# The last two turns of a pipelined transformer block written as a part of their own, with expert weights summed on TensorE

## The chip, the cores and the metric

The kernel runs on one core of one Trainium2 chip. The metric is the device time in microseconds of one execution; lower is better. Engines are named as in the profile: PE is TensorE (PEld its weight loads), DVE is VectorE, ACT is ScalarE, POOL is GpSimd and SP is the queue that issues DMAs.

## What is computed

For each of 32 batches of 256 tokens of width 128: a modulated layer norm, causal attention with 16 heads of 64 and a gated output, a residual, a second modulated layer norm, and a feed-forward part which is the sum of a gated MLP of 512 and of product-key experts. Only the experts matter here:

```python
q = (h @ Wq).reshape(b, t, 2, H, RET // 2)            # H = 4
sim = jnp.einsum('btphn,hkpn->pbthk', q, keys)        # 64 keys on each of 2 axes
sc, ix = jax.lax.top_k(sim, 8)                        # 8 of each axis
all_sc = sc[0][..., :, None] + sc[1][..., None, :]    # 64 sums, best 8 kept: scores, idx
w = silu(einsum('btd,bthkd->bthk', h, down_embed[idx])) * softmax(scores)
experts = einsum('bthk,bthkd->btd', w, up_embed[idx]) # 512 experts (NEXP)
x = x + gb * (mlp + experts)
```

## The kernel before

The 32 batches are software-pipelined. Each engine runs `body(i)` for i = -1 to 33; turns 3 to 30 are a hardware loop, the others are written out. In turn i attention works on batch i, the output projection, second norm and key similarities on f = i - 1, and the experts and the MLP on g = i - 2. So in turn 32 (i = B) there is no attention left: it finishes batch 31 up to its similarities and batch 30 wholly; turn 33 has the expert part of batch 31 alone. In both, the engines run their normal list of steps with those left out whose batch doesn't exist.

In each engine the order of the steps is the order of the calls in its list. Semaphores join the engines. Work in PSUM goes through four banks `pW[0..3]`, dealt by the list `order`: job n takes bank n modulo 4, and each job waits for the release of the one before it in its bank (`wait_free`, `filled`, `wait_full`, `release`, `wait_released`). PSUM tile `pS` holds the attention scores.

The experts are computed without a gather, over all 512 of them. With exponentials `ex` of the shifted similarities, GpSimd makes for each half batch k and head h the outer product `fsum` (8 x 64 = 512 values, `products`, L422), and from the exponentials `tops` of the best eight on each axis 20 candidates (`candidates`, L411 to L416). VectorE takes the best eight of them, their sum `zz` and its reciprocal `rz` (`thresholds`, L936 to L939). Then:

- `choose` (L948, VectorE): mask times `rz`, that is (fsum >= eighth best) * rz, into `fexp`;
- `weigh` (L431, GpSimd): `fexp` times `fsum`; `add_heads` (L438, L441): the sum over the four heads, `wsum`;
- `total` (L604, ScalarE): the sum of `wsum` over the experts, `tot`; `fold` (L447, L451, GpSimd): puts 4 - tot on the last expert and multiplies `d_t` (the silu of h times the down table, `down_tanh` L579 on ScalarE and `gated_down` L857 on VectorE) by `wsum`;
- `transpose_experts` (L1184, TensorE), its copy `eT` (`experts`, L530, ScalarE), and `project_ffn` (L1193 the MLP, L1196 the experts) into `y`; `finish` (L958, L963, VectorE) writes `yo`, which SP stores.

GpSimd also does `add_bias` (L483: `x2g`, after which SP may load the next `modB`, which `ln2_stats`, L892 to L903, needs) and `rstd2` (L473, L475), between which and `h2` (L910, `ln2_modulate`) the last batch's similarities wait. `h2` is transposed, modulated (`modulate_h`, L622), split (L630, L876) and multiplied with the keys (`similarity`); `shift` (L921, L923, L926) and `expert_exp` (L592, L598) make `ex` and `tops`. GpSimd's list in a turn is: `candidates`, `products(0)`, `products(1)`, `weigh(0)`, `add_bias`, `add_heads(0)`, `fold(0)`, `rstd2`, `weigh(1)`, `rstd1`, `add_heads(1)`, `rms1`, `fold(1)`.

Of the kernel before, what the change touches and what calls it, by code (L numbers as in the profile page):

```python
# [39 lines left out]
NW = 4  # L40
# [6 lines left out]
def program(nc, x, norm_w, Wq, Wkv, Wout, Wgate, fWg, fbg, fWu, fbu, fWd, fbd, fWq, keys,  # L47
            down, up, cond, wmod, out):
    ctx = ExitStack()
    with ctx:  # L50
# [100 lines left out]
        eT = sb("eT", [P, TB, EC, P])  # L151
        yo = sb("yo", [P, TB, D])
# [19 lines left out]
        mods_stored = sem("mods_stored")  # L172

# [60 lines left out]

        class Work:
# [17 lines left out]

            def bank(self, name, k=0):
                return pW[bank_of[name, k]]
# [12 lines left out]
            def wait_free(self, name, k=0, after=(), off=None):  # L268

                need = {}  # L270
                prev = self.before(name, k)
                for pn, pk, turn in [(*j, off) for j in after] + ([prev] if prev else []):
                    key = self.key(pn, pk)
                    need[key] = max(need.get(key, (turn, 0)), (turn, place[pn, pk] + 1))
                for key, (turn, n) in need.items():
                    e = work_free[key]
                    self.eng.wait_ge(S(e), at(e, self.i + turn, n))

            def filled(self, ins, name, k=0):
                ins.then_inc(S(work_full[self.key(name, k)]), 1)  # L280

            def wait_full(self, name, k=0, b=None):
                e = work_full[self.key(name, k)]
                self.eng.wait_ge(S(e), at(e, self.batch(name, k) if b is None else b, place[name, k] + 1))

            def release(self, ins, name, k=0):
                ins.then_inc(S(work_free[self.key(name, k)]), 1)

            def wait_released(self, name, k=0, b=None):

                e = work_free[self.key(name, k)]
                self.eng.wait_ge(S(e), at(e, self.batch(name, k) if b is None else b, place[name, k] + 1))
# [5 lines left out]
        def den(p):  # L298

            return pS[:, p % 2, :, SW:SW + TB]  # L300

# [183 lines left out]


# [19 lines left out]
        def _(act):  # L506
# [17 lines left out]
            def body(i):  # L524
# [99 lines left out]
                def high_part(high, parts, name):  # L624
                    if w.has(name):
# [4 lines left out]
                        nc.scalar.copy(parts[0][:, :], w.bank(name)[:, 0:N]).then_inc(S(high), 1)  # L630

# [332 lines left out]


# [48 lines left out]
        def _(pe):  # L1014
# [43 lines left out]
            def body(i):  # L1058
# [120 lines left out]
                def transpose_experts(k):  # L1179
                    if w.has("ET", k):  # L1180
                        pe.wait_ge(S(eo_ready[k]), at(eo_ready[k], g, 1))
# [5 lines left out]
                def project_ffn(k):  # L1187
                    if w.has("y"):
# [8 lines left out]
                        if k == TB - 1:  # L1197
                            w.filled(ins, "y")

# [83 lines left out]
```

## Time and profile before

| | us |
|---|---|
| median of 3 runs | 1504.97 |
| lowest and highest run | 1503.06, 1506.31 |
| the profiled execution | 1505.26 |
| its span, first to last instruction | 1503.5 |
| busy: PE, DVE, ACT, POOL | 1408.8, 1350.8, 1247.7, 1083.3 |
| mean granted TensorE clock | 0.981 of full |

The page cuts the span in 40 slices of 37.6 us, so the last two turns are about its last two slices. The profiled execution is one of its own, 0.3 us above the median; what the trace gives is set against its span.

### The profile page before, as it was taken

The numbers are of one execution on the slowest core, as the hardware profiler recorded it, in microseconds if no ns is written. First come the engines' busy times: TensorE is split into PE (matmuls) and PEld (weight loads), VectorE is DVE, ScalarE is ACT, GpSimd is POOL, SyncE is SP. The second block draws the span as 40 slices with busy tenths as digits, with TensorE's granted clock in tenths as the row PEclk, the third lists the DMA queues.
The fourth block names the chain that finished last, engine by engine and source line by source line (L and its number), as shares of the span: only waits on it lengthen the run. The fifth ranks groups of instructions, "written<-read, shape, count | busy, mean of one in ns | idle before, by whom it ended". The sixth has DMA issues, their size and how long they took to land.

```text
span 1503.5 us, 39396 instructions
## 1 busy us (share of the span) xinstructions
PE 1408.8 (94%) x11363; PEld 1153.2 (77%) x11363; DVE 1350.8 (90%) x5371; ACT 1247.7 (83%) x4106; POOL 1083.3 (72%) x1201
## 2 busy tenths in 40 slices
PE   6799999999999999999999999999999999999953
PEld 4678788878878887877887787888788788887743
DVE  4689999999999999999999999999999999999853
ACT  4788888898888888888888888888988888898821
POOL 0237787777778777777877777787777787777786
PEclk9999999999999999999999999999999999999976
DMA  4000000000000000000000000000000000000000
GB/s 124 19 14 20 11 14 19 19 17 18 14 9 19 19 19 16 19 14 9 19 19 19 16 19 14 9 19 19 19 16 18 9 15 19 19 16 13 12 9 6
DMA packets 50736, 27.73 MB, mean 18 GB/s; under 512 B 10288, under 2 KB 49904, under 8 KB 50704
## 3 DMA queue, kind: packets, MB, share of 16 engines
q1 hardware_dynamic: 50464, 26.91, 6.7%
q10 hardware_dynamic: 240, 0.43, 0.1%
q8 instruction: 15, 0.25, 0.1%
q14 instruction: 17, 0.14, 0.0%
HBM read 23.02 MB, written 4.31 MB: 18 GB/s over the span
## 4 chain that ended last, share of the span: by engine, by line
PE 61%; DVE 24%; issue 6%; ACT 5%; POOL 3%; DVEq 0%; DMA 0%; SPq 0%; POOLq 0%
PE pS L1115 9%; PE pW L1051 9%; PE pW L1053 7%; PE pW L1052 7%; PE pW L1128 6%; PE pS L1105 5%; DVE h L910 5%; DVE pS L828 4%; PE pS L1101 4%; ACT pS L548 4%; PE pW L1193 4%; PE pW L1196 4%; PE pW L1132 2%; DVE p_sb L848 2%; PE pW L1184 2%
## 5 line engine op out<-in xcount | busy, mean ns | idle before, releaser
L548 ACT ACTIVATE pS<-pS,nmx 128x128 f32<-128x128 f32 (+1 forms) x1024 | 391.2, 440 | 54.0 <-DVE nmx L828 54.0
L431 POOL TENSOR_TENSOR fexp<-fexp,fsum 128x512 f32<-128x512 f32 x256 | 321.0, 1288 | 80.0 <-DVE fexp L948 80.0
L828 DVE CUSTOM_DVE_ANT_0 pS<-pS,mask 128x128 f32<-128x128 f32 (+1 forms) x1024 | 330.0, 389 | 21.2 <-PE pS L1105 20.5
L422 POOL TENSOR_TENSOR fsum<-ex 128x512 f32<-128x512 f32 x256 | 258.0, 1045 | 0.0
L540 ACT COPY pT<-pS 128x768 f32<-128x768 f32 x256 | 211.7, 827 | 35.4 <-PE pS L1115 31.5
L1115 PE MATMUL pS<-ident,p_sb 128*128 128x128 f32 x1536 | 216.2, 277 | 10.4 <-DVE p_sb L848 6.4
L848 DVE TENSOR_TENSOR p_sb<-pS,coef 128x256 f32<-128x256 f32 (+2 forms) x512 | 210.4, 452 | 8.9
L1115 PEld LDWEIGHTS pS<-ident,p_sb 128*128 128x128 f32 x1536 | 172.9, 141 | 41.5 <-issue 14.8
L548 ACT ACTIVATION_READ_ACCUMULATOR pS<-pS,nmx 128x1 f32 x1024 | 200.7, 196 | 0.0
L530 ACT COPY qk<-pW 128x512 f32<-128x512 f32 x256 | 166.6, 651 | 8.0 <-PE pW L1053 8.0
L438 POOL TENSOR_TENSOR fexp<-fexp 128x512 f32<-128x512 f32 x128 | 172.5, 1368 | 0.2
L1128 PE MATMUL pW<-pT,v 128*64 128x256 f32 x1024 | 165.3, 401 | 0.4 <-ACT pT L540 0.4
L1051 PE MATMUL pW<-xT_high,s_qkv_high 128*128 128x256 f32 x512 | 156.9, 306 | 7.6 <-DVE xT_low L876 3.7
L948 DVE TENSOR_SCALAR fexp<-fsum,top,rz 128x512 f32<-128x512 f32 x256 | 162.9, 688 | 0.1
L1105 PE MATMUL pS<-qk 64*128 64x256 f32 x1024 | 155.9, 379 | 0.0
L1052 PE MATMUL pW<-xT_low,s_qkv_high 128*128 128x256 f32 x512 | 145.0, 283 | 0.0
L1053 PE MATMUL pW<-xT_high,s_qkv_low 128*128 128x256 f32 x512 | 144.8, 283 | 0.0
L828 DVE DVE_READ_ACCUMULATOR2_ANT nmx<- 128x1 f32 x1024 | 141.0, 138 | 0.0
L530 ACT COPY aoT<-pW 128x256 f32<-128x256 f32 x256 | 105.6, 412 | 42.7 <-PE pW L1132 42.4
L1101 PE MATMUL pS<-qk 64*128 64x128 f32 x1024 | 123.4, 317 | 4.0
L1156 PEld LDWEIGHTS pW<-w_out,aoT 128*128 128x128 f32 x1024 | 116.7, 192 | 10.3 <-issue 10.3
L1156 PE MATMUL pW<-w_out,aoT 128*128 128x128 f32 x1024 | 122.7, 278 | 0.0
(171 smaller groups left out, 3645.4 us busy)
## 6 DMA issues: line engine op xcount, KB each, us to landing
x_in<-in_L_attn_tokens SPq DMA_DIRECT2D x32, 128.0 KB, 2.1
x_res<-in_L_attn_tokens SPq DMA_DIRECT2D x32, 128.0 KB, 2.9
modB<-mods_dram SPq DMA_DIRECT2D x32, 128.0 KB, 2.9
out<-yo SPq DMA_DIRECT2D x32, 128.0 KB, 1.9
modA<-mods_dram SPq DMA_DIRECT2D x31, 128.0 KB, 3.0
modC<-mods_dram SPq DMA_DIRECT2D x32, 64.0 KB, 3.0
fsum<-in_L_attn_Wkv SPq DMA_DIRECT2D x2, 512.0 KB, 7.2
fsum<-in_L_attn_Wq SPq DMA_DIRECT2D x1, 512.0 KB, 5.8
```

What stands on the lines that cost most here:

```text
L422: ins = nc.gpsimd.tensor_tensor(fsum[:, k, h], ex[:, k, h, 0:NX].unsqueeze(2).broadcast_to([P, NX, NK]), ex[:, k, RH + h, :].unsqueeze(1). ...
L431: ins = nc.gpsimd.tensor_tensor(fexp[:, k, h, :], fexp[:, k, h, :], fsum[:, k, h].rearrange("p i j -> p (i j)"), ALU.mult)
L530: w.release(nc.scalar.copy(dst, src), name, k)
L548: ins = nc.scalar.activation(ps, ps, ACT.Exp, bias=nmx[:, p % 2, h, k:k + 1], scale=-1.0, accum_out=den(p)[:, h, k:k + 1])
L828: ins = nc.vector.tensor_tensor_reduce(out=ps, in0=ps, in1=mask[:, (1 - k) * P:2 * P], scale=-1.0, scalar=LARGEST, op0=ALU.add, op1=ALU.mi ...
L848: ins = nc.vector.tensor_tensor(o, pS[:, p % 2, mine, cols_of(k)], coef[:, p % 2, mine, k:k + 1].broadcast_to(o.shape), ALU.mult)
L1051: mm(o, lhs[0], rhs[0], start=True, stop=False)
L1052: mm(o, lhs[0], rhs[1], start=False, stop=False)
L1053: return mm(o, lhs[1], rhs[0], start=False, stop=True)
L1115: ins = tp(pS[:, p % 2, h, b * P:(b + 1) * P], p_sb[:, p % 2, h, b * P:(b + 1) * P], ident[:, :])
L1128: mm(bank[h * DH:(h + 1) * DH, 0:N], v[:, 0, hd], pT[:, p % 2, h, 0:2 * P], start=True, stop=False, skip_group_check=True)
L1156: ins = mm(w.bank("op")[:, k * D:(k + 1) * D], aoT[:, p, k * P:(k + 1) * P], w_out[:, p, :], start=p == 0, stop=p == NP - 1)
```

## The change

From turn 32 on every engine has a written list of its own and returns from `body` before the normal one. The loop and turns up to 31 are as they were.

- The bank deal of these turns is the list `drain`: 23 jobs with their banks given by hand, each bank with one semaphore for full and one for free.
- GpSimd does only `add_bias`, `candidates`, eight products and `rstd2` in turn 32, and `candidates`, `products(1)` and `add_bias` in turn 33. In turn 33 VectorE makes `products(0)`.
- `pick(k, h)` on VectorE gives (fsum >= eighth best) * fsum in one operation and its sum over the experts in `left`; `rest_to_last(k)` puts zz - left on the last expert of `fexp`, for each head. There is no `weigh`, `add_heads`, `total` or `fold`.
- `diagonals(k)` on ScalarE makes for each head the identity times `rz`; `turn_weights(k)` on TensorE multiplies the transpose of `fexp` by it and sums over the four heads in PSUM (`turned`, in the free `pS`), so that the weights come out scaled, summed and transposed.
- `d_t` is transposed unweighted, and `mix(k)` on VectorE multiplies `eT` by `turned`. `project_ffn` becomes `project_gated` (MLP, both halves) and `project_up(k)`.
- `gate_up(1)` stands first on TensorE and ScalarE, `project_out` ahead of `project_down(1)`; `gate_up(0)` of batch 31 still comes last in turn 32.

```diff
+        A, Z = B - 2, B - 1
+        drain = [("GU", 1, A, 2), ("PV", 6, Z, 3), ("PV", 7, Z, 0), ("D", 0, A, 1), ("op", 0, Z, 3), ("D", 1, A, 2), ("GU", 2, A, 0),
+                 ("GU", 3, A, 1), ("ET", 0, A, 2), ("hT", 0, Z, 3), ("sim", 0, Z, 0), ("sim", 1, Z, 2), ("ET", 1, A, 3), ("y", 0, A, 1),
+                 ("GU", 0, Z, 3), ("GU", 1, Z, 0), ("D", 0, Z, 2), ("D", 1, Z, 1), ("GU", 2, Z, 3), ("ET", 0, Z, 2), ("GU", 3, Z, 0),
+                 ("ET", 1, Z, 1), ("y", 0, Z, 3)]
...
+        def diag(b, k):
+            return qk[:, 2 * (b - A) + k, :].rearrange("p (h t) -> p h t", h=RH)
+        def turned(b, k):
+            return pS[:, b - A, k, :]
...
 @block.gpsimd
+                if isinstance(i, int) and i == B:
+                    add_bias()
+                    candidates()
+                    products(0)
+                    products(1)
+                    rstd2()
+                    return
+                if isinstance(i, int) and i > B:
+                    pool.wait_ge(S(rz_ready), at(rz_ready, A, 1))
+                    candidates()
+                    pool.wait_ge(pick_ready[1], RH)
+                    products(1)
+                    add_bias()
+                    return
 @block.scalar
+                def diagonals(k):
+                    act.wait_ge(S(rz_ready), at(rz_ready, g, 1))
+                    for h in range(RH):
+                        ins = nc.scalar.activation(diag(g, k)[:, h, :], ident[:, :], ACT.Copy, scale=rz[:, k, h:h + 1])
+                    ins.then_inc(diag_ready[k], 1)
                 def expert_exp(k):
...
+                        if isinstance(i, int) and i == B:
+                            act.wait_ge(S(f_ready[k]), at(f_ready[k], g, 1))
...
+                if isinstance(i, int) and i == B:
+                    gate_up(1); copy_transposes(7, -1); weighted(6); weighted(7); diagonals(0); diagonals(1)
+                    down_tanh(0); down_tanh(1); gate_up(2); gate_up(3); experts(0); modulate_h(); high_part(h2T_high, h2T, "hT")
+                    expert_exp(0); experts(1); expert_exp(1); gate_up(0)
+                if isinstance(i, int) and i > B:
+                    gate_up(1); down_tanh(0); down_tanh(1); gate_up(2); diagonals(0); diagonals(1); experts(0); gate_up(3); experts(1)
 @block.vector
+                def products(k):
+                    dve.wait_ge(S(tops_ready), at(tops_ready, g, 1))
+                    for h in range(RH):
+                        ins = nc.vector.tensor_tensor(fsum[:, k, h], ex[:, k, h, 0:NX].unsqueeze(2).broadcast_to([P, NX, NK]),
+                                                      ex[:, k, RH + h, :].unsqueeze(1).broadcast_to([P, NX, NK]), ALU.mult)
+                    ins.then_inc(product_link, 1)
+                    dve.wait_ge(product_link, 1)
+                def pick(k, h):
+                    if g == A or k == 1:
+                        dve.wait_ge(S(f_ready[k]), at(f_ready[k], g, 1))
+                    dve.wait_ge(S(rz_ready), at(rz_ready, g, 1))
+                    row = fsum[:, k, h].rearrange("p i j -> p (i j)")
+                    nc.vector.scalar_tensor_tensor(out=fexp[:, k, h, :], in0=row, scalar=top8[:, k, h, TK - 1:TK], in1=row,
+                                                   op0=ALU.is_ge, op1=ALU.mult, accum_out=left[:, k, h:h + 1]).then_inc(pick_ready[k], 1)
+                def rest_to_last(k):
+                    seen = (g - A) * (RH + 1)
+                    dve.wait_ge(pick_ready[k], seen + RH)
+                    nc.vector.tensor_tensor(left[:, k, :], zz[:, k, :], left[:, k, :], ALU.subtract).then_inc(fix_link, 1)
+                    dve.wait_ge(fix_link, (g - A) * TB + k + 1)
+                    last = fexp[:, k, :, NE - 1]
+                    nc.vector.tensor_tensor(last, last, left[:, k, :], ALU.add).then_inc(pick_ready[k], 1)
+                def mix(k):
+                    w.wait_released("ET", k)
+                    dve.wait_ge(turned_full[k], g - A + 1)
+                    o = eT[:, k].rearrange("p c t -> p (c t)")
+                    nc.vector.tensor_tensor(o, o, turned(g, k), ALU.mult).then_inc(mixed_ready[k], 1)
+                if isinstance(i, int) and i == B:
+                    bias_product(1); gate_product(1); thresholds(); pick(0,0); pick(0,1); pick(0,2); gated_down(0); pick(0,3)
+                    rest_to_last(0); gated_down(1); pick(1,0); ln2_stats(); pick(1,1); bias_product(2); gate_product(2)
+                    ln2_modulate(); bias_product(3); gate_product(3); pick(1,2); low_part(h2T_high, h2T, "hT"); pick(1,3); rest_to_last(1)
+                    mix(0); shift(0); shift(1); mix(1); finish(); bias_product(0); gate_product(0)
+                if isinstance(i, int) and i > B:
+                    products(0); bias_product(1); gate_product(1); gated_down(0); thresholds(); pick(0,0); pick(0,1); pick(0,2); pick(0,3); rest_to_last(0)
+                    gated_down(1); pick(1,0); pick(1,1); pick(1,2); pick(1,3); rest_to_last(1); bias_product(2); gate_product(2); mix(0)
+                    bias_product(3); gate_product(3); mix(1); finish()
 @block.tensor
                 def transpose_experts(k):
...
+                        if isinstance(i, int) and i >= B:
+                            w.wait_released("D", k, g)
+                        else:
+                            pe.wait_ge(S(eo_ready[k]), at(eo_ready[k], g, 1))
...
+                def turn_weights(k):
+                    seen = (g - A) * (RH + 1)
+                    pe.wait_ge(S(pT_ready), at(pT_ready, Z, NP - 1 + g - A))
+                    pe.wait_ge(diag_ready[k], g - A + 1)
+                    o = turned(g, k)
+                    for h in range(RH):
+                        pe.wait_ge(pick_ready[k], seen + h + 1)
+                        for c in range(EC - 1):
+                            mm(o[:, c * P:(c + 1) * P], fexp[:, k, h, c * P:(c + 1) * P], diag(g, k)[:, h, :],
+                               start=h + c == 0, stop=h == RH - 1, skip_group_check=True)
+                    pe.wait_ge(pick_ready[k], seen + RH + 1)
+                    for h in range(RH):
+                        ins = mm(o[:, (EC - 1) * P:], fexp[:, k, h, (EC - 1) * P:], diag(g, k)[:, h, :],
+                                 start=False, stop=h == RH - 1, skip_group_check=True)
+                    ins.then_inc(turned_full[k], 1)
+                def project_gated():
+                    w.wait_free("y", 0, after=[("GU", c) for c in range(FC)], off=-2)
+                    for k in range(TB):
+                        o = w.bank("y")[:, k * D:(k + 1) * D]
+                        for c in range(FC):
+                            mm(o, g_t[:, c, k * P:(k + 1) * P], w_d[:, c, :], start=k + c == 0, stop=False, skip_group_check=True)
+                def project_up(k):
+                    pe.wait_ge(mixed_ready[k], g - A + 1)
+                    o = w.bank("y")[:, k * D:(k + 1) * D]
+                    for c in range(EC):
+                        ins = mm(o, eT[:, k, c, :], w_up[:, c, :], start=False, stop=c == EC - 1, skip_group_check=True)
+                    if k == TB - 1:
+                        w.filled(ins, "y")
+                if isinstance(i, int) and i == B:
+                    gate_up(1); transpose_scores(7, -1); weigh_values(6); weigh_values(7); project_down(0); project_out()
+                    project_down(1); gate_up(2); turn_weights(0); gate_up(3); transpose_experts(0); transpose_h(); similarity(0)
+                    similarity(1); turn_weights(1); transpose_experts(1); project_gated(); project_up(0); project_up(1); gate_up(0)
+                if isinstance(i, int) and i > B:
+                    gate_up(1); project_down(0); project_down(1); gate_up(2); transpose_experts(0); turn_weights(0); gate_up(3)
+                    transpose_experts(1); turn_weights(1); project_gated(); project_up(0); project_up(1)
```

In the code the lists stand one call a line; several are set in a line here. `drained` makes `bank`, `wait_free`, `filled`, `wait_full`, `release` and `wait_released` use the new semaphores for the jobs of `drain`.

## Rows read from the trace of the kernel before

**Rows 1.** The page: granted clock in 40 slices; the landing of one DMA.
```profile
...
PEclk9999999999999999999999999999999999999976
...
modB<-mods_dram SPq DMA_DIRECT2D x32, 128.0 KB, 2.9
...
```

**Rows 2.** Windows of turns 31, 32, 33: length; busy PE, PEld, DVE, ACT, POOL; clock.
```profile
...
1382.20:1425.00 42.80, 42.54 (x354) 35.41 (x353) 37.78 (x155) 37.92 (x128) 32.08 (x34) 1.00 0.05 12
1425.00:1463.20 38.20, 23.32 (x143) 19.12 (x141) 21.82 (x63) 12.69 (x29) 32.46 (x35) 0.73 0.03 10
1463.20:1503.50 40.30, 13.77 (x73) 12.07 (x71) 14.64 (x32) 6.83 (x16) 26.48 (x24) 0.66 0.03 9
...
```

**Rows 3.** Waits in the last 78 us: total, times, longest.
```profile
...
ACT junk L604 <- POOL wsum L441: 26.9, 4, 9.9
...
PE pW L1184 <- POOL d_t L451: 18.7, 2, 10.2
...
DVE pW L892 <- DMA modB<-mods_dram: 3.8, 1, 3.8
...
```

**Rows 4.** The chain of waits, last 60 us: start, duration, what.
```profile
...
1445.85 2.50 DVE h L910 x2
...
1458.51 0.30 ACT tops L598
...
1459.82 8.02 POOL fsum L422 x8
...
1469.58 5.34 POOL fexp L431 x4
...
1482.31 4.89 POOL fexp L431 x4
...
1493.71 1.11 PE pW L1184 x4
...
1500.76 0.42 DVE yo L963
```

**Rows 5.** Groups of VectorE by form, whole run: busy us, mean ns.
```profile
...
L828 DVE CUSTOM_DVE_ANT_0 pS<-pS,mask 128x256 f32<-128x256 f32 x512 | 236.3, 461 | 0.0
...
L828 DVE DVE_READ_ACCUMULATOR2_ANT nmx<- 128x1 f32 x1024 | 141.0, 138 | 0.0
...
L857 DVE SCALAR_TENSOR_TENSOR d_t<-d_t,pW 128x512 f32<-128x512 f32 x64 | 43.2, 676 | 0.5 <-ACT d_t L579 0.5
...
```

**Rows 6.** Groups of ScalarE by form, whole run.
```profile
...
L592 ACT ACTIVATE ex<-sh 128x512 f32<-128x512 f32 x64 | 41.0, 640 | 0.5 <-DVE sh L923 0.5
...
L610 ACT ACTIVATE xr<-h,rr 128x128 f32<-128x128 f32 x64 | 22.0, 395 | 0.6 <-POOL rr L467 0.6
...
```

**Rows 7.** Timeline of TensorE: start, duration, what, count.
```profile
...
1434.68 3.73 PE L1156 MATMUL pW<-w_out,aoT 128*128 128x128 f32 x32
...
1450.67 0.76 PE L1051 MATMUL pW<-s_sim_high,h2T_high 128*128 128x512 f32 x1 [1.58 <-DVE h2T_low L876]
...
1462.39 1.06 PE L1196 MATMUL pW<-w_up,eT 128*128 128x128 f32 x8
...
1494.62 1.91 PE L1193 MATMUL pW<-w_d,g_t 128*128 128x128 f32 x8
...
```

**Rows 8.** `top_d` on VectorE from 1200 us on: shortest, median, longest ns.
```profile
...
L926 DVE TENSOR_TENSOR top_d<-top_s x7: 281/1351/1354, 1200.5 to 1457.9; 128x128 f32<-128x128 f32 x7
...
```

**Rows 9.** Timeline of VectorE.
```profile
...
1425.90 0.42 DVE L963 TENSOR_TENSOR yo<-pW,x2g 128x256 f32<-128x256 f32 x1
...
1428.37 0.41 DVE L870 SCALAR_TENSOR_TENSOR g_t<-g_t,pW 128x256 f32<-128x256 f32 x1
...
1440.98 0.43 DVE L892 TENSOR_TENSOR pW<-pW,modB 128x256 f32<-128x256 f32 x1 [3.78 <-DMA modB<-mods_dram]
...
```

**Rows 10.** Timeline of GpSimd.
```profile
...
1421.29 0.31 POOL L411 TENSOR_TENSOR cand<-tops 128x64 f32<-128x64 f32 x1 [0.24 <-ACT tops L598]
...
```

**Rows 11.** Timeline of the SP queue: when a DMA is issued.
```profile
...
1438.05 0.34 SPq L366 DMA_DIRECT2D modB<-mods_dram  x1
...
```

More of the change, by code:

```diff
@@ L151, in program @@
         eT = sb("eT", [P, TB, EC, P])
+        left = sb("left", [P, TB, RH])
         yo = sb("yo", [P, TB, D])
@@ L268, in wait_free @@
             def wait_free(self, name, k=0, after=(), off=None):
+                job = self.drained(name, k, self.batch(name, k))
+                if job:
+                    for pn, pk in after:
+                        self.wait_released(pn, pk, self.i + off)
+                    n, count_n = job
+                    if count_n > 1:
+                        self.eng.wait_ge(drain_free[n], count_n - 1)
+                    else:
+                        pn, pk, turn = [j for m, j in enumerate(order) if m % NW == n and j[2] <= 0][-1]
+                        self.wait_released(pn, pk, B - 1 + turn)
+                    return
                 need = {}
@@ new lines, in body @@
+                if isinstance(i, int) and i == B:
+                    bias_product(1)
+                    gate_product(1)
+                    thresholds()
+                    pick(0, 0)
+                    pick(0, 1)
+                    pick(0, 2)
+                    gated_down(0)
+                    pick(0, 3)
+                    rest_to_last(0)
+                    gated_down(1)
+                    pick(1, 0)
+                    ln2_stats()
+                    pick(1, 1)
+                    bias_product(2)
+                    gate_product(2)
+                    ln2_modulate()
+                    bias_product(3)
+                    gate_product(3)
+                    pick(1, 2)
+                    low_part(h2T_high, h2T, "hT")
+                    pick(1, 3)
+                    rest_to_last(1)
+                    mix(0)
+                    shift(0)
+                    shift(1)
+                    mix(1)
+                    finish()
+                    bias_product(0)
+                    gate_product(0)
+                    return
@@ new lines, in body @@
+                if isinstance(i, int) and i > B:
+                    products(0)
+                    bias_product(1)
+                    gate_product(1)
+                    gated_down(0)
+                    thresholds()
+                    pick(0, 0)
+                    pick(0, 1)
+                    pick(0, 2)
+                    pick(0, 3)
+                    rest_to_last(0)
+                    gated_down(1)
+                    pick(1, 0)
+                    pick(1, 1)
+                    pick(1, 2)
+                    pick(1, 3)
+                    rest_to_last(1)
+                    bias_product(2)
+                    gate_product(2)
+                    mix(0)
+                    bias_product(3)
+                    gate_product(3)
+                    mix(1)
+                    finish()
+                    return
```

100 lines of the change are left out of this document (94 added, 6 removed).

## The prediction

> **What bounds the kernel now.** The page's slices come first [rows 1]. TensorE has its full clock in all slices but the last two of 40. The change touches only code after the loop (turns B = 32 and B+1 = 33 of `body`), so the question is what the last 80 us wait for. The windows, cut where turn 32 and turn 33 begin, show it [rows 2]: the last two turns take 38.2 and 40.3 us, nearly as long as a full turn (42.8), although TensorE's work is down to 23.3 and 13.8 us. GpSimd alone keeps 32.5 and 26.5 us. The table of waits names the same engine [rows 3]: ScalarE waited 26.9 us for `wsum` and TensorE 18.7 us for `d_t`, both made by GpSimd. VectorE also waited 3.8 us for the DMA of `modB`. The chain of waits then gives the order [rows 4]: `tops` of the last batch is ready at 1458.8; eight products take 8.0 us, four `weigh` multiplications 5.3, heads, total, fold and `d_t` bring it to 1482.3, four more `weigh` 4.9, and only at 1493.7 may TensorE turn the last `d_t`. The output is written at 1501.2, so the last batch's expert part costs 42.4 us from `tops` to `yo`. Before it, the same GpSimd list stands ahead of `rstd2`: `h2` of the last batch is ready only at 1448.35 [rows 4].
>
> **What is removed and what replaces it.** For each of the last two batches GpSimd loses `weigh`, `add_heads` and `fold`; ScalarE loses `total`; VectorE's sixteen `choose` become sixteen `pick` (eight for each batch). New are: sixteen small scaled copies of the identity on ScalarE, 64 matmuls 128x128 of four-byte data on TensorE (16 for each half batch), `rest_to_last` and `mix` on VectorE, and in turn 33 four of the eight products on VectorE.
>
> **Prices.** A `pick` is scalar_tensor_tensor over 512 elements with an accumulator; no row has this form. From below it costs the same operation without accumulator, 0.676 us [rows 5], of which successive instructions overlap about 0.08. From above it costs that plus the 0.138 us of an accumulator read, 0.81. The 256-wide operation with accumulator takes 0.461 [rows 5] and its read overlaps the next operation, so I take 0.67. VectorE's products and `mix` are priced by the same row: 0.65. `rest_to_last`: two tiny operations and two semaphores, 0.45 (0.3 to 0.6). A copy of the identity: 0.395 at most [rows 6], 0.33 taken because successive ones overlap; four are 1.3 us. A 128x128 matmul: eight took 1.06 us at granted clock 2.4 GHz and 1.91 at 1.2 GHz, about 0.11 and 0.21 each [rows 7]; sixteen are 1.8 or 3.4 us.
>
> **A lock between two engines.** `top_d`, 128x128 with two inputs in SBUF, takes 0.281 us while GpSimd is idle and 1.35 in the median [rows 8]: it waits until GpSimd's running instruction is over. `h2` (L910) shows the same, 2.5 us for two small operations [rows 4]. A `pick` has two SBUF inputs, so I let picks and GpSimd's products alternate. The Trainium skill, "SBUF — State Buffer", "Who interferes with whom", says that a VectorE instruction with two SBUF inputs and a GpSimd instruction that reads SBUF exclude each other for their whole length; by that rule, the trace agrees; without it the sum below would be 1.4 us shorter.
>
> **Turn 32, step by step.** Up to 1428.8, where VectorE's last `gate_product(0)` ends [rows 9], nothing changes except GpSimd's start. There `add_bias` is now first, and it waits for `yo` of the batch before, which ends at 1426.3 [rows 9]; `candidates`, at 1421.3 before [rows 10], moves behind it. So: 1426.3 + 0.75 + 0.95 for candidates + four products at 1.0 = 1432.1. This late start is a loss of 5.8 us on GpSimd, but its list behind it is short now. VectorE has `bias_product(1)`, `gate_product(1)` (0.9) and `thresholds` (1.25) done at 1431.7, so the first pick waits only 0.4. The other four products (4.0) alternate with three picks (2.0): GpSimd is done at 1438.1. Then pick 0.67, rest 0.45, `gated_down` 0.6, pick 0.67: 1440.5. `ln2_stats` follows. TensorE's projection took 3.73 us from 1434.7 [rows 7]; with `gate_up(1)` earlier and `project_down(1)` later it ends at about 1436.1, no limit. Its `modB` is no limit either: the SP queue issues this DMA once `x2g` is ready, now about 1427.3 instead of 1438.05 [rows 11], and it lands 2.9 us later [rows 1]. The wait of 3.8 us goes, but VectorE's own queue takes over until 1440.5, against 1441.0 before [rows 9]. The large gain is behind it: 1.7 for the statistics, 1.2 on an idle GpSimd, and 0.6 for `h2` instead of 2.5, with pick(1,1) and `bias_product(2)` in the gaps (0.4 lost): `h2` at 1444.2 against 1448.35, a gain of 4.1.
> Behind `h2` the trace takes 2.2 us to the start of the first `sim` matmul [rows 7]: 1446.4. TensorE then has, in its order, two `sim` groups (1.7 and 1.3 at 1.2 GHz), the 16 matmuls of `turn_weights(1)` (3.4) and four transposes (0.9): 1453.7. The ScalarE queue has `experts(1)` ahead of `expert_exp(1)`, so `tops` waits for these transposes: two operations 512 wide at 0.64 [rows 6], less 0.1 of overlap each, and 0.3 for `tops` [rows 4] give 1455.1. Before it was 1458.8 [rows 4]. Turn 32 gives 3.7 us; part of the 4.1 is spent on TensorE.
>
> **Turn 33.** TensorE adds 16 matmuls of `y` at 1.2 GHz (3.4): 1457.1; `finish` 0.9; `gate_up(0)`, queued behind it on TensorE, passes ScalarE at 1458.8, and its two products end on VectorE at 1459.8. From here VectorE has the longest list: four products 2.6 (GpSimd does the other four by 1460.1, so there is hardly a collision), GU 1 0.9, `gated_down` 0.6, `thresholds` 1.25, four picks 2.7, rest 0.45, `gated_down` 0.6, four picks 2.7, rest 0.45, GU 2 0.9, `mix(0)` 0.6, GU 3 0.9: 14.65, so 1474.5. `turn_weights(1)` starts after pick, transposes and `gate_up(3)` at about 1471.8 and ends at 1475.2 at the low clock. Then 16 matmuls of `y`, 3.4: 1478.7; 0.1 and `finish` 0.85: 1479.6. The low clock is taken because TensorE ran the last batch's `y` at 0.21 us a matmul after a gap [rows 7], and here it again has gaps of several us while VectorE picks. From `tops` to `yo` this makes 24.5 us instead of 42.4.
> The output DMA behind it stays, 2.3 us from the end of `yo` to the end of the span. Sum: 3.7 + 17.9 = 21.6 us. The profiled execution has 1505.26 us for a span of 1503.5 and is 0.3 above the median, so the new median is 1504.97 - 21.6 = 1483.4, **1483 us**.
>
> **Where I could be wrong, with prices.**
> *Forecast, 0.5:* the sum, 1479 to 1487. Its own parts, a few tenths each way in sixteen picks and a dozen handovers, make about 4 us.
> *Faster, 0.2:* TensorE regains 2.4 GHz in both turns and the picks don't exclude products. Then `tops` waits for VectorE's `shift(1)` instead of TensorE (2.4 us earlier), the end of the turn saves 2.4, the lock 1.4: 6.2, **1477**. For it: the trace's clock rose again within turn 32 of before, where `y` was busy (1.06 us for eight) [rows 7]. Against it: the row on `top_d` [rows 8] and the gaps that the picks leave.
> *Less gain, 0.26:* turn 32 yields nothing, because TensorE's extra matmuls and the late start of GpSimd's products eat the 3.7 us: 1487; with picks at 0.81 (16 x 0.14 = 2.2) 1489. For it: ScalarE's queue order puts `experts(1)` before the exponential on which the last batch hangs. Against it: `h2` is freed from GpSimd.
> *Slower than before, 0.02:* one mechanism, the pick. If the accumulating form ran slowly, every pick would be paid on VectorE, eight in turn 32 and eight in turn 33. To eat 21.6 us it would have to cost 0.67 + 21.6/16 = 2.0 us; at 2.5 us the time would be 1512. The accumulating rows, 0.461 us for 256 elements [rows 5], speak against it.
> *No change, 0.02:* the picks and copies queue so that each waits for a whole list of another engine and the last two turns stay at 80 us: 1505. The 18.7 us which TensorE waited for `d_t` would have to reappear as waits for `fexp` or `diag`, and no list in turn 33 is that long.
> The range takes in the sums of the fast and the slow case: 1476 to 1490, outside of which I leave about 1.5 in 10. A difference of 0.2% (3 us) can be told from none; faster 0.96, same 0.02, slower 0.02.
>
> **What the changed profile will show.** The last slices: GpSimd nearly idle at the end. The chain of waits in the last 25 us: VectorE with `fexp`, then TensorE `pW`; no GpSimd after the last products. `modB`'s wait gone. `h2` at about 1444, `tops` at about 1455, a pick at about 0.67 us, and those of the first half of turn 32 spaced by 1.6. TensorE's granted clock in the last 20 us near half. The forecast is wrong if `tops` is not before 1458, if picks cost over 0.8, or if ScalarE's diagonals hold `down_tanh(0)` so long that VectorE waits at `gated_down(0)` for more than 1 us: eight copies end at about 1434.4 and the tanh at 1435.0, while VectorE comes to it at 1437.1, so a cover of 2 us hides them.

## The result, and the profile after

The changed kernel takes 1485.08 us in the median of four runs (1484.75 to 1487.4), against 1504.13 before in the same comparison: a ratio of 0.9875, with a 95% interval of 0.9863 to 0.9887. It is faster by about 19 us. The forecast was 1483, between 1476 and 1490.

The windows answer to [rows 2]. The turns are cut near where `finish` of the turn before begins on VectorE, as there. Turn 32 takes 31.4 us instead of 38.2 and turn 33 26.8 instead of 40.3; GpSimd's busy time falls from 32.5 and 26.5 us to 14.1 and 4.2, and TensorE's clock is 0.95 and 0.87 of full instead of 0.73 and 0.66. In the last 21.2 us, the third line, GpSimd does nothing and the clock is 0.84:

```profile
...
1425.00:1456.40 31.40, 26.90 (x212) 24.54 (x210) 24.50 (x78) 13.93 (x37) 14.11 (x20) 0.95 0.05 13
1456.40:1483.20 26.80, 18.44 (x137) 17.29 (x135) 18.05 (x50) 7.72 (x20) 4.24 (x5) 0.87 0.05 13
1462.00:1483.20 21.20, 14.60 (x110) 14.06 (x110) 13.50 (x43) 4.23 (x12) 0.00 (x0) 0.84 0.02 7
...
```

The chain of waits answers to [rows 4]. In turn 32 it runs through GpSimd only from `add_bias` to the first four products (1427.1 to 1432.7) and in `rstd2` (1442.1 to 1443.5). In turn 33 it is VectorE's from 1458.3 up to `rz` of the last batch at 1465.1, then ScalarE's for the first four `diagonals`, and behind them TensorE's, with `turn_weights` (L1405, L1409) and the projections (L1418, L1424), up to `finish`:

```profile
...
1428.68 4.01 POOL fsum L475 x4
...
1434.17 1.02 DVE fexp L1085 x2
...
1443.50 0.60 DVE h L1017 x2
...
1449.02 2.72 PE pS L1405 x24
...
1454.86 1.79 PE pW L1424 x16
...
1459.13 3.27 DVE fsum L1075 x4
...
1465.15 1.29 ACT qk L705 x4
...
1466.53 4.31 PE pS L1405 x24
...
1472.90 2.68 PE pS L1405 x24
...
1476.47 1.79 PE pW L1418 x16
1478.26 1.80 PE pW L1424 x16
...
1480.55 0.42 DVE yo L1070
```

The SP queue answers to [rows 11]; the 3.8 us which VectorE waited for `modB` [rows 3] are gone:

```profile
...
1428.25 0.34 SPq L419 DMA_DIRECT2D modB<-mods_dram  x1
...
```

The profiled executions are of the same code up to turn 31, yet VectorE's last `gate_product(0)` of turn 31 (L870 before, L977 after) ends at 1428.8 in the one before and at 1429.3 after, and between 1425.6 and 1428.3 in the experiments below. From that point on, which is called the mark below, steps that have the same code repeat within 0.1 us where TensorE's clock doesn't enter. So the kernels are compared by distances read from VectorE's and ScalarE's timelines: from the mark to `h2` and to `tops`, from `tops` to the last `yo`, and the sum of these two.

| kernel | to `h2` | to `tops` | `tops` to `yo` | sum | median, us | ratio to before, 95% interval |
|---|---|---|---|---|---|---|
| before | 19.6 | 30.0 | 42.4 | 72.4 | 1504 | |
| changed | 14.8 | 25.1 | 26.6 | 51.6 | 1485.1 | 0.9863 to 0.9887 |
| e1 add_bias last | 13.6 | 24.2 | 26.7 | 51.0 | 1481.7 | 0.9837 to 0.9868 |
| e2 second input in PSUM | 13.4 | 24.2 | 27.0 | 51.2 | 1482.7 | 0.9839 to 0.9866 |
| e3 turn 32 alone | 14.8 | 23.8 | 41.7 | 65.4 | 1499.6 | 0.9954 to 0.9976 |
| e4 MLP products early | 14.8 | 26.5 | 29.4 | 55.9 | 1486.5 | 0.9866 to 0.9896 |
| e5 unread matmuls, turn 33 | 14.8 | 26.4 | 25.2 | 51.5 | 1483.0 | 0.9848 to 0.9878 |
| e6 e4 with unread matmuls | 14.8 | 25.4 | 25.9 | 51.2 | 1482.7 | 0.9848 to 0.9878 |
| e7 float32r | 14.8 | 23.3 | 27.1 | 50.4 | 1481.8 | 0.9841 to 0.9871 |
| e8 e1 and e7 | 13.6 | 22.3 | 27.3 | 49.7 | 1479.9 | 0.9826 to 0.9853 |
| e9 unread matmuls, both turns | 14.8 | 23.8 | 25.2 | 48.9 | 1480.4 | 0.9830 to 0.9857 |
| e10 e8, e6 and e9 together | 13.6 | 21.6 | 25.1 | 46.7 | 1476.2 | 0.9798 to 0.9825 |
| e11 e10 without unread matmuls | 13.6 | 23.4 | 26.0 | 49.4 | 1480.6 | 0.9824 to 0.9851 |

Of the 20.8 us between the first two rows, 4.9 lie ahead of `tops` and 15.8 behind it. The executions differ by up to 3.7 us in when the unchanged code reaches the mark, so small differences are read from the distances, and each of these comes from one profiled execution. They have a spread of their own: the changed kernel, e4, e5 and e6 have the same code up to `tops` and took 25.1, 26.5, 26.4 and 25.4 us to it, and e3, whose turn 32 has the same code too, took 23.8. With the same turn 33 the changed kernel, e1 and e2 took 26.6, 26.7 and 27.0 us behind `tops`. Differences smaller than these are not shown by a single pair of executions.

### The profile page after: what moved, and what is told of

Its sections match the earlier page's. It is cut to its first block, busy times and chain, and to the rows that moved or that the text cites. A ratio compares the mean times of both kernels' runs of the same rounds, so it can differ in the third digit from the quotient of the medians.

```text
span 1483.2 us, 39666 instructions
## 1 busy us (share of the span) xinstructions
PE 1415.4 (95%) x11491; PEld 1162.9 (78%) x11491; DVE 1356.4 (91%) x5403; ACT 1247.8 (84%) x4114; POOL 1037.8 (70%) x1161
## 3 DMA queue, kind: packets, MB, share of 16 engines
HBM read 23.02 MB, written 4.31 MB: 18 GB/s over the span
## 4 chain that ended last, share of the span: by engine, by line
PE 63%; DVE 25%; issue 6%; ACT 5%; DMA 1%; POOL 0%; DVEq 0%; SPq 0%; POOLq 0%
PE pS L1309 9%; PE pW L1245 9%; PE pW L1247 7%; PE pW L1246 7%; PE pW L1322 6%; PE pS L1299 5%; DVE h L1017 5%; DVE pS L935 4%; PE pS L1295 4%; ACT pS L616 4%; PE pW L1393 4%; PE pW L1390 4%; PE pW L1326 2%; DVE p_sb L955 2%; PE pW L1381 2%
## 5 line engine op out<-in xcount | busy, mean ns | idle before, releaser
L484 POOL TENSOR_TENSOR fexp<-fexp,fsum 128x512 f32<-128x512 f32 x240 | 300.3, 1284 | 76.8 <-DVE fexp L1055 76.8
L491 POOL TENSOR_TENSOR fexp<-fexp 128x512 f32<-128x512 f32 x120 | 162.2, 1372 | 0.1
L1055 DVE TENSOR_SCALAR fexp<-fsum,top,rz 128x512 f32<-128x512 f32 x240 | 149.7, 676 | 0.0
```

The lines of the kernel that those rows point to most:

```text
L484: ins = nc.gpsimd.tensor_tensor(fexp[:, k, h, :], fexp[:, k, h, :], fsum[:, k, h].rearrange("p i j -> p (i j)"), ALU.mult)
```

## The experiments

GU 0 to GU 3 are the four parts of the gated MLP: `gate_up(c)` on TensorE and ScalarE, then `bias_product(c)` and `gate_product(c)` on VectorE. A record is one line of TensorE's in the profile. The granted clock is 1.00 at 2.4 GHz and 0.50 at 1.2 GHz; values between are means over a stretch.

**Turn 32 alone (e3).** Turn 33 runs the normal lists on the new banks:

```diff
-                if isinstance(i, int) and i > B:
+                if False:
...
-                        pool.wait_ge(S(masks_ready), at(masks_ready, g, k + 1))
+                        pool.wait_ge(S(masks_ready), at(masks_ready, seq(i), k + 1))
```

The first edit is made on all four engines; the second, with `seq(i)` one less than g in turn 33, for each semaphore that turn 32 no longer raises.

> Turn 32 as in the changed kernel, turn 33 with the normal lists (choose, weigh, add_heads, total, fold) on the new bank deal. Theory 1 (the two turns' gains add: 4.9 us in turn 32 up to tops, 15.8 from tops to yo): about 1485.1 + 15.8 = 1501, tops to yo 42 us. Theory 2 (the new deal and order of turn 32 are what pays, since turn 33 starts with its GU work done): below 1495. Theory 3 (turn 32 alone loses, because the early products and TensorE's extra work delay turn 33's first steps): 1504 or more.

From `tops` to `yo` it takes 41.7 us, as before (42.4), and the chain is GpSimd's again:

```profile
...
1451.12 8.37 POOL fsum L479 x8
...
1460.32 5.29 POOL fexp L488 x4
...
1473.01 4.89 POOL fexp L488 x4
...
```

The sum is 65.4, 7.0 less than before, but the profiled execution is the fastest of the seven (1495.85 us); the median is 1499.6, 4.8 below the 1504.4 of before. Theory 1 had 1501. So the gains of the two turns add as far as the spread lets one see, and in this execution turn 32 came out 1.3 us better than inside the change: while TensorE did `turn_weights(1)` and what surrounds it, its granted clock was 1.00 in e3 and 0.80 in the changed kernel (windows of 5 us).

**GpSimd's late start (e1), and the second SBUF input by itself (e2).**

In e1 GpSimd's list of turn 32 is

```diff
-                    add_bias()
                     candidates()
                     products(0)
                     products(1)
+                    add_bias()
                     rstd2()
```

and in e2 the second input of turn 32's picks comes from PSUM:

```diff
                     row = fsum[:, k, h].rearrange("p i j -> p (i j)")
-                    nc.vector.scalar_tensor_tensor(out=fexp[:, k, h, :], in0=row, scalar=top8[:, k, h, TK - 1:TK], in1=row,
+                    if g == A:
+                        dve.wait_ge(S(pT_ready), at(pT_ready, Z, NP))
+                    second = pS[:, 1, 0, :] if g == A else row
+                    nc.vector.scalar_tensor_tensor(out=fexp[:, k, h, :], in0=row, scalar=top8[:, k, h, TK - 1:TK], in1=second,
```

> In turn 32 GpSimd does add_bias behind the eight products instead of ahead of them; nothing else differs from the changed kernel. Theory 1 (the late start of GpSimd costs time): candidates start at about 1421.8 instead of 1427.7, both product groups are done by 1431, before the first pick; the picks of half 0 take 0.67 us apart instead of 1.45, GpSimd's eight products 8.05 us instead of 9.4; VectorE then waits for down_tanh(0) and (1) and reaches ln2_stats at about 1439.0 instead of 1440.2: 1.2 us less, about 1484. Theory 2 (VectorE's queue up to ln2_stats is set by TensorE's project_out ahead of project_down(1), not by GpSimd): below 0.3 us less. Theory 3 (the modB DMA comes back as the bound): a wait for modB in front of ln2_stats and a time above 1486.

> In turn 32 the second input of each pick is read from PSUM (old scores) instead of SBUF, so the weights of batch 30 are not those of the reference; the work and the order are the same. Theory 1 (two SBUF inputs exclude GpSimd's products): picks of half 0 are 0.67 to 0.75 us apart instead of 1.45, GpSimd's eight products take 8.05 us instead of 9.4, ln2_stats starts about 1.2 us earlier. Theory 2 (the accumulating form is slow next to a busy GpSimd, or the product's rate is what spaces the picks): picks stay 1.45 apart and nothing changes.

The timeline of VectorE in turn 32, the changed kernel first. The three picks are 1.45 us apart and each is charged with its wait:

```profile
...
1432.72 1.51 DVE L1085 SCALAR_TENSOR_TENSOR fexp<-fsum,top 128x512 f32<-128x512 f32 x1 [0.74 <-POOL fsum L475]
...
1434.17 1.52 DVE L1085 SCALAR_TENSOR_TENSOR fexp<-fsum,top 128x512 f32<-128x512 f32 x1
...
1435.62 1.52 DVE L1085 SCALAR_TENSOR_TENSOR fexp<-fsum,top 128x512 f32<-128x512 f32 x1
...
1440.17 0.43 DVE L999 TENSOR_TENSOR pW<-pW,modB 128x256 f32<-128x256 f32 x1
...
```

With the second input in PSUM they are 0.67 apart, at the same late start of GpSimd:

```profile
...
1431.45 0.75 DVE L1088 SCALAR_TENSOR_TENSOR fexp<-fsum,top,pS 128x512 f32<-128x512 f32 x1 [0.74 <-POOL fsum L475]
...
1432.12 0.74 DVE L1088 SCALAR_TENSOR_TENSOR fexp<-fsum,top,pS 128x512 f32<-128x512 f32 x1
...
1432.79 0.74 DVE L1088 SCALAR_TENSOR_TENSOR fexp<-fsum,top,pS 128x512 f32<-128x512 f32 x1
...
1437.70 0.43 DVE L999 TENSOR_TENSOR pW<-pW,modB 128x256 f32<-128x256 f32 x1
...
```

GpSimd's eight products, in the changed kernel and in e2:

```profile
...
1428.64 9.40 POOL L475 TENSOR_TENSOR fsum<-ex 128x512 f32<-128x512 f32 x8
...
```

```profile
...
1427.37 8.05 POOL L475 TENSOR_TENSOR fsum<-ex 128x512 f32<-128x512 f32 x8
...
```

The products lose 9.40 - 8.05 = 1.35 us beside the picks, and three picks lose about 0.8 us each. Both lengthenings go when one of the two SBUF inputs goes, so it is the second SBUF input and not the form of the instruction. In e1 the picks no longer meet the products: these take 8.05 us and end at 1427.7, before the first pick at 1429.0, and the first three picks start 0.67 apart. In both `ln2_stats` starts 9.6 us after the mark instead of 10.8, the 1.2 us which theory 1 of each gave, and ahead of it ScalarE's tanh has become the wait (0.8 us in front of `gated_down(1)` in both; that tanh had itself waited 1.95 us for TensorE's `project_down(1)`). No wait for `modB` came back in e1. At `tops` 0.9 is left and at `yo` 0.5 to 0.7, both less than the spread above, so what the collision costs at the end is not settled. e1 and e2 agree so closely up to `ln2_stats` (9.64 and 9.63) that GpSimd's late start costs nothing there apart from the collision.

**The order in turn 33 (e4), and its clock (e5, e6).**

In e4 VectorE's turn 33 has, behind `products(0)`, `thresholds`, GU 1 and GU 2, then the picks with GU 3 between those of half 0, and both `mix` last; ScalarE has `gate_up(3)` ahead of the diagonals; TensorE's list is

```diff
                     gate_up(2)
+                    gate_up(3)
                     transpose_experts(0)
+                    project_gated()
                     turn_weights(0)
-                    gate_up(3)
                     transpose_experts(1)
                     turn_weights(1)
-                    project_gated()
                     project_up(0)
```

e5 leaves the changed kernel's order and adds matmuls whose result nobody reads:

```diff
+                def keep_busy(n):
+                    pe.wait_ge(mixed_ready[0], 1)
+                    for _ in range(n):
+                        mm(pS[:, 0, 0, :], h2T[0][:, 0:P], s_down[0][:, :], start=True, stop=True)
...
                     gate_up(2)
+                    keep_busy(16)
                     transpose_experts(0)
+                    keep_busy(6)
                     turn_weights(0)
```

e6 is e4 with `keep_busy(17)` behind `gate_up(2)`, `keep_busy(4)` behind `transpose_experts(0)` and `project_gated` behind `turn_weights(0)`.

> In turn 33 the MLP products GU 2 and GU 3 are done on VectorE ahead of the picks, thresholds ahead of GU 1, and TensorE runs gate_up(3) and project_gated before turn_weights(0), so that only project_up stands behind the last mix; all work is the same. Theory 1 (the end is set by TensorE's queue behind the last rest_to_last): project_gated's 1.8 us and part of the wait of mix(1) leave the end, yo about 3 us earlier, about 1482. Theory 2 (VectorE's list as a whole is the bound): 1 us or less. Theory 3 (TensorE falls to 1.2 GHz in the longer gaps and runs turn_weights(1), 32 records, at 0.21 each): no gain or a loss.

> The changed kernel with 22 matmuls whose result nobody reads (512 wide, one record each) in TensorE's two gaps of turn 33: 16 behind gate_up(2), 6 behind transpose_experts(0). Theory 1 (the fall of TensorE's clock after the 3.9 us gap is what makes turn_weights(0) end at 1471.5, and everything behind it late): transposes and turn_weights(0) run at 0.11 us a record, turn_weights(0) ends with the picks at about 1469, turn_weights(1) about 2 us earlier, from candidates to yo 1.5 to 2 us less than the 26.6 of the changed kernel. Theory 2 (VectorE's list of turn 33 is the bound): TensorE runs faster and the end moves by 0.3 us at most. Theory 3 (the clock does not follow these matmuls): records of turn_weights(0) still 0.2 us.

> The order with the MLP products early, with 21 unread matmuls in TensorE's gaps of turn 33 and project_gated behind turn_weights(0) instead of ahead of it. Theory 1 (that order lost only by the low clock and by project_gated standing ahead of turn_weights(0)): TensorE at 0.11 us a record through turn 33, mix(1) ends about 1.6 us behind the last rest_to_last, yo 1.9 us behind that; from tops to yo about 24 us, 5 less than with that order alone and 2.5 less than the changed kernel. Theory 2 (the order is worse by itself, because thresholds and picks begin later behind GU 1 to 3): 26.5 us or more.

e4 lost 2.9 us behind `tops`. Theory 3 had a loss by the low clock, but in `turn_weights(1)`, which ran at 0.11 us a record. TensorE's timeline shows where it was lost: it waits 4.38 us for a bank, runs at 0.21 us a record after that, and `project_gated`, now ahead of `turn_weights(0)`, waits for GU 3 and takes 3.75 us:

```profile
...
1464.36 0.58 PE L1245 MATMUL pW<-h2T_high,s_g_high 128*128 128x256 f32 x1 [4.38 <-DVE g_t L977]
...
1468.22 3.75 PE L1418 MATMUL pW<-w_d,g_t 128*128 128x128 f32 x16 [1.23 <-DVE g_t L977]
1471.77 3.98 PE L1405 MATMUL pS<-qk,fexp 128*128 128x128 f32 x24
...
```

e5 keeps the order and fills the gap. The changed kernel's `turn_weights(0)` and e5's, same stretch of TensorE's timeline:

```profile
...
1464.12 1.08 PE L1381 MATMUL pW<-ident,d_t 128*128 128x128 f32 x4 [3.88 <-DVE d_t L964]
1466.53 4.31 PE L1405 MATMUL pS<-qk,fexp 128*128 128x128 f32 x24 [1.33 <-ACT qk L705]
...
```

```profile
...
1462.58 0.63 PE L1381 MATMUL pW<-ident,d_t 128*128 128x128 f32 x4 [0.24 <-DVE d_t L964]
...
1464.99 2.92 PE L1405 MATMUL pS<-qk,fexp 128*128 128x128 f32 x24 [0.39 <-ACT qk L705]
...
```

24 records take 2.92 us instead of 4.31, and `tops` to `yo` 25.2 instead of 26.6: 1.4 us, a little under theory 1's 1.5 to 2. Its sum is not lower, because in that execution turn 32, whose code is the same, happened to run more at the low clock (`tops` at 26.4 instead of 25.1). e6 shows that the clock and the place of `project_gated` together, which it doesn't separate, explain e4's loss, but the order is no gain: 25.9, against e5's 25.2 with the clock at 1.00 in both. Theory 1 had 24 and theory 2 26.5 or more. The last `rest_to_last` ends 1.65 us later (19.25 behind `tops` instead of 17.60), which is theory 2's mechanism.

**The clock in both turns (e9).**

Turn 33 is as in e5 (with other operands for the unread matmuls), and TensorE's turn 32 has

```diff
                     transpose_experts(0)
+                    keep_busy(8)
                     transpose_h()
+                    keep_busy(6)
                     similarity(0)
```

> The changed kernel with unread matmuls in TensorE's gaps of both turns (8 and 6 in turn 32, around the transposes of h2; 16 and 6 in turn 33). Theory 1 (the low clock costs time in both turns): the two similarity groups of turn 32 run at 0.23 us a record instead of 0.43, tops 1.5 us earlier than the 25.1 us of the changed kernel (counted from the last gate_product(0) of turn 31), and turn 33 as with its unread matmuls alone, 25.2 us; together about 49 us instead of 51.6. Theory 2 (VectorE's shift and ScalarE's queue bound tops): tops 0.3 us earlier at most.

The windows around `similarity` and the picks of turn 33, the changed kernel first; the granted clock is the number behind the five pairs of busy time and count:

```profile
...
1442.00:1449.00 7.00, 3.82 (x14) 2.77 (x13) 6.65 (x24) 2.22 (x5) 1.28 (x2) 0.76 0.00 1
...
1464.00:1471.50 7.50, 6.05 (x37) 5.71 (x37) 7.33 (x28) 2.92 (x9) 0.00 (x0) 0.64 0.00 0
...
```

```profile
...
1438.50:1444.00 5.50, 5.41 (x26) 4.04 (x25) 5.30 (x16) 2.23 (x5) 1.29 (x2) 1.00 0.00 1
...
1459.00:1466.00 7.00, 6.38 (x49) 5.78 (x49) 6.83 (x27) 2.92 (x9) 0.00 (x0) 1.00 0.01 2
...
```

With 36 unread matmuls the clock stays at 1.00 throughout, `tops` comes at 23.8 and `yo` 25.2 behind it: 48.9, 2.7 us less than the change, and the expected 49. In turn 33 the low clock costs 1.4 us: e5 and e9 both took 25.2, and the three executions without unread matmuls 26.6 to 27.0. In turn 32 it costs 1.3 us against the changed kernel's execution. That it is the clock fits e3, where it was 1.00 in the same stretch without any unread matmul and `tops` came at 23.8 too; against e4 and e5 it would be 2.6 to 2.7. The Trainium skill ("TensorE: Matmul & The Clock Gate", "What's actually happening") says that the low clock is the normal state and activity lifts it; the two windows agree, 0.64 against 1.00 with the same useful work of TensorE.

**TensorE's work (e7), and with GpSimd's order (e8).** The picks and the scaled identities are written as float32r, so the weights are rounded to that type (`pick`, `rest_to_last` and `turn_weights` use `fexp_r` for `fexp`):

```diff
+        fexp_r = sb("fexp_r", [P, TB, RH, NE], F32R)
...
         def diag(b, k):
-            return qk[:, 2 * (b - A) + k, :].rearrange("p (h t) -> p h t", h=RH)
+            n = 2 * (b - A) + k
+            return s_qkv[0][:, n * RH * P:(n + 1) * RH * P].rearrange("p (h t) -> p h t", h=RH)
```

> turn_weights on float32r data: the picks are written as float32r, the scaled identities too (in the dead s_qkv), so that each of its 64 matmuls is one short record instead of two long ones; the weights are rounded to that type. Theory 1 (TensorE is the bound behind both turns' last picks): a turn_weights of 3.6 us at the high clock falls to about 1 us; tops come about 2.5 us earlier, mix(1) of turn 33 follows VectorE's list without its wait of 2.25 us; together 4 to 5 us less than the changed kernel. Theory 2 (VectorE's lists are the bound): 2.5 us less at most, all of it in turn 32. Theory 3 (picks written as float32r are slower on VectorE): picks above 0.8 us and no gain.

> Both float32r in turn_weights and add_bias behind the products. Theory 1 (the two costs lie on one chain one behind the other, so that they add): from VectorE's last gate_product(0) of turn 31 to yo 1 us less than with float32r alone. Theory 2 (with shorter matmuls another wait, on ScalarE's tanh or its queue, swallows it): 0.3 us or less.

The groups of `turn_weights` by form in the last two turns, the changed kernel and e7 (busy us, mean ns of one):

```profile
...
L1405 PE MATMUL pS<-qk,fexp 128*128 128x128 f32 x96 | 12.9, 297 | 1.3 <-ACT qk L705 1.3
L1409 PE MATMUL pS<-qk,fexp 128*128 128x128 f32 x32 | 4.2, 275 | 0.0
...
```

```profile
...
L1407 PE MATMUL pS<-s_qkv_high,fexp_r 128*128 128x128 f32 x48 | 8.8, 348 | 1.6 <-ACT s_qkv_high L707 1.6
...
L1411 PE MATMUL pS<-s_qkv_high,fexp_r 128*128 128x128 f32 x16 | 3.4, 348 | 0.0
...
```

The 64 matmuls of float32 are 128 records; those of float32r are 64, and one is not shorter: at the high clock, in turn 32 of e7, twelve took 1.40 us from the first to what follows, 0.12 each. So the work of a call halves, from 3.6 to 1.8 us; I had expected about 1. The unread float32r matmuls of e5, 512 columns wide, follow each other every 0.23 us: four times the columns in twice the time. So at 128 columns it is not the columns that set the pace; what does was not tried. `tops` came 1.8 us earlier at the same granted clock (0.79 in the 4 us from 18 us behind the mark, in both), but behind it nothing was won: 27.1 instead of 26.6. With less to do TensorE stays at the low clock there. The same stretch behind `tops`, the changed kernel first:

```profile
...
1463.90:1475.90 12.00, 10.45 (x75) 10.11 (x76) 10.12 (x37) 4.23 (x12) 0.00 (x0) 0.77 0.01 1
...
```

```profile
...
1459.00:1471.00 12.00, 10.13 (x48) 9.81 (x49) 10.17 (x38) 4.34 (x12) 0.00 (x0) 0.52 0.00 0
...
```

Expected were 4 to 5 us and 1.3 came. Behind `tops`, what the shorter records give, the clock takes back: `mix(1)` starts 21.4 us behind `tops` instead of 22.2, but from there to the start of `finish` it takes 4.8 us instead of 3.5. e8 takes 0.7 off e7, between its two theories (1 and 0.3).

**All of it (e10, e11).** e10 has add_bias last, float32r, e6's order and unread matmuls in both turns; e11 the same without the unread matmuls.

> add_bias behind the products, float32r in turn_weights, the MLP products early in turn 33, unread matmuls in TensorE's gaps of both turns. Theory 1 (three costs on one chain: the port, TensorE's time, its clock): from the last gate_product(0) of turn 31 to yo about 46 us instead of 51.6, tops at about 21.8 and yo 24 us behind. Theory 2 (they overlap, and VectorE's list is the bound behind each of them): 48.5 or more, little better than the 49.7 of float32r with add_bias moved.

> As the combination, without the unread matmuls. Theory 1 (the clock is a cost of its own): 1.5 to 3 us slower than the combination with them. Theory 2 (with short records TensorE is no bound at either clock): within 0.5 us of it.

e10 gives 46.7, near theory 1's 46, and 1476.15 us in the median: 0.9812 of before (0.9798 to 0.9825), faster than both kernels. e11 gives 49.4, 2.7 us more, and 1480.57 in the median, so the clock is a cost of its own even with short records. Of the 2.7 us, 1.8 lie ahead of `tops` and 0.9 behind it. Behind `tops` the unread matmuls did not hold the clock in e10's profiled execution. In this window of turn 33 TensorE is busy throughout, almost all of it at the low clock:

```profile
...
1459.30:1464.30 5.00, 5.00 (x24) 4.60 (x21) 4.90 (x16) 2.70 (x9) 0.00 (x0) 0.52 0.00 0
...
```

In e6, with the same order and as many unread matmuls there, it stayed at 1.00. e10's gap behind the first 17 of them was longer (a wait of 1.19 us for GU 1's `g_t` instead of 0.51), which may be why but was not tried. The order is not settled: e8 and e11 differ only in turn 33, where e11 took 26.0 us and e8 27.3, but their medians are 0.9838 and 0.9840 of before. With the clock at 1.00 and float32 the same order lost 0.7 us (e6 against e5).

## Why the prediction was right, and where it wasn't

The direction, the place and the mechanism were right: `weigh`, `add_heads` and `fold` left the end of both turns; e3 shows that turn 33's gain goes when they come back. That the sum came within 2 us is in part luck: two terms for TensorE were wrong in opposite directions, as the fourth point below shows.

- *Turn 32 up to `h2`.* Forecast 15.4 us after the mark, measured 14.8; a pick costs 0.67 from start to start, as taken. Behind the start of `ln2_stats` the text's own terms add to 3.9 us where it took 3.7, and 3.9 was measured. The lock made the picks of half 0 1.45 apart (forecast 1.6), and GpSimd lost 0.45 us for each. e1 and e2 show it worth 1.2 us up to `ln2_stats`, near the 1.4 that the text gave; at the end 0.5 to 0.7 was read, which the spread doesn't let one tell from none or from all of it.
- *Up to `tops`.* Forecast 26.3, measured 25.1. The order that I used is the trace's: `sim`, `turn_weights(1)`, transposes, ScalarE's `experts(1)`, `tops`.
- *From `tops` to `yo`.* Forecast 24.5, measured 26.6. The whole distance was forecast as 50.8 (72.4 less 21.6) and measured as 51.6. In spans of the profiled executions the forecast is 1481.9 and the measured 1483.2: 0.8 us of the difference is this distance, and 0.56 the loop, which ended that much later.
- **The step that failed is the price of a 128x128 matmul.** I read "eight took 1.06 us" as eight matmuls. The eight records of [rows 7] are four matmuls of float32, two records each, as the loops over FC = 4 and EC = 4 in `project_ffn` would have told me, and as the 128 records for 64 matmuls after show. `turn_weights` is 3.6 us at the high clock, not 1.8, and the last `y` likewise. The forecast survived because a second term erred the other way: I took 1.2 GHz for `turn_weights(1)` and `y` in both turns, and they ran mostly at 2.4 (3.6 us each in turn 33, from 1472.9 and from 1476.5). The text also named a granted clock near half in the last 20 us; it was 0.84 in the last 21. That the doubled work itself kept the clock up fits e7, where half of it left the clock at 0.52 instead of 0.77, but it is one pair of executions. Where the clock was low as I had it, at `turn_weights(0)` of turn 33, the mis-sized term came through: 5.2 us, so that `turn_weights(1)` ended 22.1 us behind `tops` instead of 20.1. Those are the missing 2 us; the next two points have a share in them.
- *VectorE's list of turn 33* was 17.6 us from `tops` to the last `rest_to_last` against 17.0 by the forecast: its four products took 3.26 instead of 2.6, beside GpSimd's `add_bias`. The text took it for the longest list of the turn. Up to `rz` it is the chain, but behind it TensorE is: VectorE waits 2.25 us for TensorE before `mix(1)` and 2.81 before `finish`.
- *Diagonals* cost 0.31 us each. In turn 32 they lie hidden: `down_tanh(0)` ends at 1435.1 and VectorE comes to `gated_down(0)` at 1437.1, the cover of 2 us that the text gave. In turn 33 they don't, and the text put them at nothing: the first four stand on the chain for 1.29 us, and `turn_weights(0)` starts at 1466.5 although the first pick ended at 1465.9. By these two rows they cost about 0.6 us there, an estimate that no run tried. `modB` was issued at 1428.25 and no one waited for it.
- *The rivals.* The faster one's mechanisms are both real, but smaller than its 6.2 us: the clock 2.7 (e9), the lock 1.2 at most (e1, e2). Less gain: turn 32 gave 4.9 us up to `tops` in the changed kernel, and e3's median is 4.8 us below before, so it did not happen. The slow pick did not happen.

Not settled: why turn 32, with the same code, shows `tops` between 25.1 and 26.5 us in four executions and 23.8 in a fifth (e3). The clock of TensorE around `similarity` differs in them: in the 4 us from 18 us behind the mark it was 0.50 in e4 and e5 (`tops` at 26.5 and 26.4), 0.72 in e6 (25.4), 0.79 in the changed kernel (25.1) and 1.00 in e3 (23.8). e9's one execution, with unread matmuls and 1.00, has 23.8 as well. What sets the clock from one execution to the next I have not tried to show.

## What to carry to other kernels

Read the drain of a pipelined kernel as a kernel of its own: its lists were made for turns in which other work hides the waits, and here the chain ran through GpSimd, which was busy for only 32.1 of the 42.8 us of turn 31 [rows 2]. When a trace is used as a price list, count its records against the source's calls before you divide. Shorter work on an engine whose clock follows its activity may give little back until the clock is held too; measure the two together. And look at the waits for another engine's small steps, as the diagonals here: hidden in one turn, they stood on the chain in the next.

## What the runs showed of the hardware

- A float32 128x128 matmul stands as two records of 0.11 us at 2.4 GHz; a float32r one as one record of 0.12 us (e7), so it is twice as fast at this size. Float32r matmuls of 512 columns follow each other every 0.23 us (e5).
- A VectorE operation with two SBUF inputs and GpSimd's products hold each other up: 1.45 us instead of 0.67 for each of three picks, and 9.40 instead of 8.05 us for GpSimd's eight products. With one of the two inputs in PSUM neither is held up (e2).
- With unread matmuls of 512 columns in TensorE's gaps the granted clock was 1.00 in stretches in which it otherwise stood at 0.64 and 0.76 (e5, e6, e9). In e10 it fell all the same, to 0.52 in turn 33.
